# Row maxima of an attention kernel: block-diagonal matmuls become row tiles, and the spread of the inverse moves

## The reference

```
q = heads(x @ Wq.T)
k, v = heads(text @ Wk.T), heads(text @ Wv.T)
k_ip, v_ip = heads(ip @ Wk_ip.T), heads(ip @ Wv_ip.T)
out = softmax(q k^T / sqrt(32)) v + softmax(q k_ip^T / sqrt(32)) v_ip
y = merge(out) @ Wo.T + bo + x
```

## Time and profile before

| | us |
|---|---|
| median of three runs | 685.42 (683.55 to 728.46) |
| the profiled execution | 683.04 |
| its span | 681.2 |

### The profile page before, as it was taken

One profiled execution on the slowest core, in us unless ns is written; L12 is line 12 of the kernel. 1 busy time (PEld: TensorE's weight loads), 2 busy tenths in 40 slices (PEclk: granted clock), 3 DMA queues, 4 the chain that ended last, 5 costly groups with the idle time before them and its releaser, 6 DMA issues.

```text
span 681.2 us, 18904 instructions
## 1 busy us (share of the span) xinstructions
PE 657.5 (97%) x6514; PEld 564.5 (83%) x6514; DVE 435.7 (64%) x956; ACT 493.3 (72%) x1078; POOL 225.0 (33%) x261
## 2 busy tenths in 40 slices
PE   9959798999999999999999999999999999999997
PEld 9959576788888888888888888888888888888877
DVE  6786677675757566675756576665657566756633
ACT  3983787877868777877777787778777777876730
POOL 4020102243432434343434324343434243342333
PEclk9989898999999999999999999999999999999999
DMA  8950111223131221313131312213131323212212
GB/s 318 410 234 9 25 56 34 80 57 96 49 103 51 82 63 55 93 48 97 51 93 49 99 55 86 55 55 93 48 101 51 90 55 93 56 50 64 56 42 69
DMA packets 34691, 57.46 MB, mean 84 GB/s; under 512 B 4832, under 2 KB 27232, under 8 KB 34400
## 3 DMA queue, kind: packets, MB, share of 16 engines
q1 hardware_dynamic: 34656, 56.99, 27.3%
HBM read 35.34 MB, written 10.49 MB: 67 GB/s over the span
## 4 chain that ended last, share of the span: by engine, by line
PE 85%; DVE 6%; ACT 6%; issue 2%; POOL 0%; DVEq 0%; ACTq 0%
PE q_ps L711 19%; PE x_ps L711 19%; PE sum_ps L769 11%; PE b_ps L752 10%; PE pv_ps L780 10%; PE a_ps L735 7%; PE x_ps L789 5%; PE a_ps L741 1%; ACT probs L405 1%; DVE k_stack L631 1%; DVE k_stack L641 1%; ACT k_stack L485 1%; ACT q_stack L397 1%; DVE wo_lo L554 1%; DVE k_stack L545 1%
## 5 line engine op out<-in xcount | busy, mean ns | idle before, releaser
L405 ACT ACTIVATE probs<-b_ps 77x512 f32<-77x512 f32 x320 | 181.1, 591 | 121.0 <-PE b_ps L752 119.3
L562 DVE TENSOR_TENSOR q_stack<-q_ps,q_hi 32x256 fp32r<-32x256 f32 x320 | 134.3, 420 | 36.0 <-ACT q_hi L390 32.3
L571 DVE TENSOR_REDUCE row_max<-a_ps 128x4 f32<-128x308 f32 x320 | 137.6, 471 | 24.0 <-PE a_ps L735 21.3
L397 ACT ACTIVATE q_stack<-q_hi 32x256 fp32r<-32x256 f32 x320 | 133.0, 416 | 10.0
L598 DVE TENSOR_TENSOR scaled<-x_ps,pv_sb 128x512 f32<-128x512 f32 x75 | 51.9, 692 | 105.4 <-PE x_ps L789 105.0
L752 PE MATMUL b_ps<-q_stack,k_stack 98*77 98x256 f32 x640 | 115.1, 281 | 0.5 <-ACT probs L405 0.5
L347 POOL TENSOR_TENSOR scaled<-scaled 128x256 f32<-128x256 f32 x80 | 59.2, 740 | 139.1 <-DVE scaled L598 139.0
L352 POOL TENSOR_TENSOR attn_lo<-scaled,attn_hi 128x256 fp32r<-128x256 f32 x80 | 59.1, 739 | 113.2 <-ACT attn_hi L434 113.2
L358 POOL TENSOR_TENSOR res<-y,res 128x256 f32<-128x256 f32 x70 | 51.1, 731 | 136.8 <-ACT y L428 136.8
L735 PE MATMUL a_ps<-k_diag,q_hi 128*128 128x308 f32 x320 | 87.3, 313 | 7.0 <-DVE row_max L571 6.8
L752 PEld LDWEIGHTS b_ps<-q_stack,k_stack 98*77 98x77 f32 x640 | 85.7, 146 | 1.5 <-ACT probs L405 1.0
(11 more groups left out here) (111 smaller groups left out, 962.3 us busy)
## 6 DMA issues: line engine op xcount, KB each, us to landing
x_raw<-x_in SPq DMA_DIRECT2D x16, 640.0 KB, 4.2
q_stack<-q_stack SPq DMA_DIRECT2D x80, 128.0 KB, 2.3
res<-x_in SPq DMA_DIRECT2D x75, 128.0 KB, 2.0
y_out<-res SPq DMA_DIRECT2D x75, 128.0 KB, 1.7
stage<-wk_in SPq DMA_DIRECT2D x6, 640.0 KB, 7.9
...
```

Source lines behind the costliest of these rows:

```text
L397: done = nc.scalar.activation(q_stack[0:D, u.slot, j, :], q_hi[j * D:(j + 1) * D, u.slot, :].bitcast(F32), ACT.Copy)
L405: nc.scalar.activation(probs[0:KEYS, j, :], b_ps[j % 2][0:KEYS, :], ACT.Exp).then_inc(b_drained, 1)
L562: done = nc.vector.tensor_tensor(q_stack[D:2 * D, u.slot, j, :], q_ps[rows, 0:N], q_hi[rows, u.slot, :].bitcast(F32), ALU.subtract)
L571: nc.vector.tensor_reduce(row_max[:, u.slot, br, :, sub], bank[:, 0:BLK].rearrange("p (j n) -> p j n", j=GROUP), AXIS.X, ALU.max).then_inc ...
```

## The change

The block-diagonal keys are replaced by `k_heads`, in which each head keeps its own 32 rows, with the 77 keys of both branches side by side. The maxima of a unit become eight matmuls of 154 columns: for each half of the queries four, one a head, each on its own row tile of 32 rows and into its own PSUM bank (b_ps0, b_ps1, a_ps0, a_ps1). They stand at the end of a unit, behind the weighted values, for the unit two ahead. VectorE reduces a bank at a time, at the start of its unit, ahead of `normalise`. The query projection is cut into pieces of 5, 3, 4 and 3 steps between the scores. The transposition and then the spread (now into a_ps1) follow the last score, ahead of the output projection. `normalise` and POOL's `add_branches` take the unit five back in place of six; ScalarE's four exponentials stand together behind `keep_pv`, `keep_sums` and `attn_high`.

```diff
-BLK = GROUP * KEYS
+BLK = BRANCHES * KEYS
...
-MAXES = SUB * BRANCHES
-A_ITEMS = MAXES + 1
+MAX_ITEMS = GROUP + 1
...
-        k_diag = sbuf("k_diag", [P, BRANCHES, GROUPS, BATCHES, GROUP, KEYS], F32R)
+        k_heads = sbuf("k_heads", [P, GROUPS, BATCHES, BRANCHES, KEYS], F32R)
...
+        max_banks = [*b_ps, *a_ps]
...
-                ahead, norm, chunk = u.tile_plus(1), u.plus(-1 - SPREAD_LAG), u.plus(-OUT_LAG)
+                ahead, norm, chunk = u.tile_plus(1), u.plus(-SPREAD_LAG), u.plus(-OUT_LAG)
+                if norm.plus(-1).exists():
+                    attn_low(norm.plus(-1))
                 if norm.exists():
                     add_branches(norm)
-                    attn_low(norm)
...
                 before, ahead, nxt = u.tile_plus(-1), u.tile_plus(2), u.plus(2)
                 norm, chunk = u.plus(-1 - SPREAD_LAG), u.plus(-OUT_LAG)
-                exp(u, 0)
-                exp(u, 1)
                 if u.plus(-1).exists():
                     keep_pv(u.plus(-1))
                 if u.g == 0 and before.exists():
                     keep_sums(before)
-                exp(u, 2)
                 if norm.exists():
                     attn_high(norm)
-                exp(u, 3)
+                for j in range(GROUP):
+                    exp(u, j)
                 if nxt.exists():
                     q_high(nxt)
                     q_top(nxt)
...
-                for j in range(GROUP):
-                    rows = slice(j * D, (j + 1) * D)
-                    done = nc.scalar.activation(
-                        k_diag[rows, br, g, :, j, :],
-                        k_banks[br][g % 2][rows, group_cols(g)].rearrange("p (b n) -> p b n", b=BATCHES),
-                        ACT.Copy, scale=SCALE)
-                done.then_inc(k_hi_done, 1)
+                nc.scalar.activation(k_heads[:, g, :, br, :],
+                                     k_banks[br][g % 2][:, group_cols(g)].rearrange("p (b n) -> p b n", b=BATCHES),
+                                     ACT.Copy, scale=SCALE).then_inc(k_hi_done, 1)
...
-            def max_piece(u, k):
-
-                sub, br = divmod(k, BRANCHES)
-                wait(dve, a_ready, u.number(A_ITEMS, k + 1))
-                bank = a_ps[(u.c * A_ITEMS + k) % 2]
-                nc.vector.tensor_reduce(row_max[:, u.slot, br, :, sub],
-                                        bank[:, 0:BLK].rearrange("p (j n) -> p j n", j=GROUP), AXIS.X,
-                                        ALU.max).then_inc(a_drained, 1)
+            def max_piece(u, j, bank):
+
+                if not (u.fixed and u.number() == 0):
+                    wait(dve, max_ready, u.number(1, 1))
+                nc.vector.tensor_reduce(row_max[:, u.slot, :, j, :].rearrange("p r s -> p s r"),
+                                        bank[:, 0:SUB * BLK].rearrange("p (s r n) -> p s r n", s=SUB, r=BRANCHES),
+                                        AXIS.X, ALU.max).then_inc(max_read, 1)
 
             def max_turned(u):
 
-                wait(dve, a_ready, u.number(A_ITEMS, A_ITEMS))
+                wait(dve, max_turned_over, u.number(1, 1))
                 wait(dve, max_in[u.slot], u.uses_of_slot(DMA) - DMA)
                 nc.vector.tensor_copy(max_rows[:, u.slot, :],
-                                      a_ps[(u.c * A_ITEMS + MAXES) % 2][0:BRANCHES * SUB * GROUP, 0:P]).then_inc(a_drained, 1)
+                                      a_ps[0][0:BRANCHES * SUB * GROUP, 0:P]).then_inc(max_read, 1)
...
-            def normalise(u, bank=x_ps):
+            def normalise(u, bank=a_ps[1]):
...
             def emit(u):
-                norm, nxt = u.plus(-1 - SPREAD_LAG), u.plus(1)
-                if norm.exists():
+                norm, nxt = u.plus(-SPREAD_LAG), u.plus(1)
+                if nxt.exists():
+                    if not (u.fixed and u.number() == 0):
+                        for j in range(GROUP):
+                            max_piece(nxt, j, max_banks[j])
+                    max_turned(nxt)
+                if norm.exists() and u.g != 0:
                     normalise(norm)
-                if nxt.exists():
-                    for k in range(MAXES):
-                        max_piece(nxt, k)
-                    max_turned(nxt)
                 if u.g == 0 and u.tile_plus(-1).exists():
                     invert_sums(u.tile_plus(-1))
+                if norm.exists() and u.g == 0:
+                    normalise(norm)
                 if u.plus(2).exists():
                     q_low(u.plus(2))
...
-            def max_scores(u, k):
-
-                sub, br = divmod(k, BRANCHES)
-                if k == 0:
-                    wait(pe, q_hi_done, u.number(1, 1))
-                wait(pe, a_drained, u.number(A_ITEMS, k - 1))
-                nc.tensor.matmul(a_ps[(u.c * A_ITEMS + k) % 2][:, 0:BLK], q_hi[:, u.slot, sub * P:(sub + 1) * P],
-                                 k_diag[:, br, u.g, u.batch].rearrange("p j n -> p (j n)"),
-                                 start=True, stop=True).then_inc(a_ready, 1)
+            def max_matmuls(u, heads, banks):
+
+                for sub in range(SUB):
+                    for j, bank in zip(heads, banks):
+                        rows = slice(j * D, (j + 1) * D)
+                        done = nc.tensor.matmul(bank[:, sub * BLK:(sub + 1) * BLK],
+                                                q_hi[rows, u.slot, sub * P:(sub + 1) * P],
+                                                k_heads[rows, u.g, u.batch].rearrange("p r n -> p (r n)"),
+                                                start=True, stop=True, skip_group_check=True)
+                return done
+
+            def max_scores(u):
+
+                wait(pe, q_hi_done, u.number(1, 1))
+                wait(pe, max_read, u.number(MAX_ITEMS))
+                wait(pe, scaled_done, u.number(1, -1 - SPREAD_LAG))
+                max_matmuls(u, range(GROUP), max_banks).then_inc(max_ready, 1)
 
             def turn_maxima(u):
-                wait(pe, a_drained, u.number(A_ITEMS, MAXES))
-                nc.tensor.transpose(a_ps[(u.c * A_ITEMS + MAXES) % 2][0:BRANCHES * SUB * GROUP, 0:P],
-                                    row_max[:, u.slot].rearrange("p r j s -> p (r j s)"), ident[:]).then_inc(a_ready, 1)
+                wait(pe, max_read, u.number(MAX_ITEMS, GROUP))
+                nc.tensor.transpose(a_ps[0][0:BRANCHES * SUB * GROUP, 0:P],
+                                    row_max[:, u.slot].rearrange("p r j s -> p (r j s)"), ident[:]
+                                    ).then_inc(max_turned_over, 1)
...
                     wait(pe, max_in[u.slot], u.uses_of_slot(DMA))
+                if j < 2 and u.plus(1).exists():
+                    wait(pe, max_read, u.number(MAX_ITEMS, MAX_ITEMS + j + 1))
                 wait(pe, b_drained, u.number(GROUP, j - 1))
...
                 wait(pe, scaled_done, u.number())
-                wait(pe, y_done, u.number(1, 1 + SPREAD_LAG - OUT_LAG))
-                spread_matmuls(u, x_ps)
+                if u.plus(SPREAD_LAG + 1).exists():
+                    wait(pe, max_read, u.number(MAX_ITEMS, (SPREAD_LAG + 1) * MAX_ITEMS + GROUP))
+                spread_matmuls(u, a_ps[1])
 
             def project_out(c):
 
-                wait(pe, scaled_done, c.number(1, OUT_LAG - SPREAD_LAG))
+                wait(pe, y_done, c.number())
                 out_chunk(c, x_ps)
 
...
-
-                def find_max(k):
-                    if nxt.exists():
-                        max_scores(nxt, k) if k < MAXES else turn_maxima(nxt)
-
-                find_max(0)
-                find_max(1)
+                project_q(u.plus(2), 0, 5)
                 scores(u, 0)
+                project_q(u.plus(2), 5, 8)
                 scores(u, 1)
-                project_q(u.plus(2), 0, 8)
-                find_max(2)
+                project_q(u.plus(2), 8, 12)
                 scores(u, 2)
-                find_max(3)
-                project_q(u.plus(2), 8, 10)
+                project_q(u.plus(2), 12)
                 scores(u, 3)
-                project_q(u.plus(2), 10, 13)
-                find_max(MAXES)
-                project_q(u.plus(2), 13)
+                if nxt.exists():
+                    turn_maxima(nxt)
+                if norm.exists():
+                    spread_inverse(norm)
                 if chunk.exists():
                     project_out(chunk)
                 row_sums(u)
                 weigh_values(u)
-                if norm.exists():
-                    spread_inverse(norm)
+                if u.plus(2).exists():
+                    max_scores(u.plus(2))
...
-            max_scores(first, 0)
-            max_scores(first, 1)
+            wait(pe, q_hi_done, 1)
+            max_matmuls(first, (0, 1), a_ps).then_inc(first_max_ready, 1)
             project_ip_values(4, 5)
-            max_scores(first, 2)
-            max_scores(first, 3)
+            wait(pe, max_read, 2)
```

(4 more changed lines are left out.)

29 lines of the change are left out of this document (14 added, 15 removed).

## The result

| | before | after |
|---|---|---|
| median | 685.07 us (4 runs, 683.55 to 728.46) | 783.57 us (4 runs, 781.88 to 786.82) |
| profiled execution, span | 683.04, 681.2 | 781.88, 780.0 |

The change makes the kernel slower: the ratio is 1.145, with a 95% interval of 1.140 to 1.151. One of the four executions of the kernel before, 728.46, fell in a slower state and is not in the ratio. The prediction had the direction and, of the mechanisms, the largest one, but 735 us and an upper end of 770 are both too low.

The account below looks back on a forecast made before the run. TensorE, busy 97% of the span, was taken to bound the steady part. 683 - 4 (prologue) - 2 (first ten units) - 13 (maxima) + 47 (spread) + 3 (third score) + 21 (clock) = 735 us, range 705 to 770.

Parts of the forecast that it names:

- the term of -2 for the first ten units: First ten units, bound by ScalarE and VectorE: their order shortens a little, 2 us saved (0 to 5).
- nothing, as long as these margins of 0.05 us and more hold: Moved waits in an ordinary unit: each result is ready before TensorE needs it, so no cost.
- Maxima: Maxima block on TensorE: 0.56 us removed, 0.18 added plus 0.20 for leaving row tiles; 13 us saved over 70 units.
- The first is the thinnest: Margin at a unit's first score: maxima piece read at 0.65 us, score stands at 0.7; each 0.1 us is 8 us.
- The spread in mid-unit: In a tile's first unit TensorE's spread waits 3.15 us for VectorE's inverse of the sums, 15 times: 47 us.
- The clock after such a wait: After each wait for the inverse TensorE's granted clock drops: 1.4 us for 15 tiles, 21 us, bounds 0 and 26.
- Rival A: The clock holds at the stalls where the spread waits: 714 us in place of 735; chance 0.14.
- The third score of a tile's first unit: A tile's first exponential comes 0.4 us late behind ScalarE's split of x; third score waits 0.2, 15 times: 3 us.
- The prologue: Before the first units: fewer ScalarE copies for scaled keys, TensorE's wait for x_lo ends near 43; 4 us saved.
- Rival C: In the maxima block, row tiles load one after another: 0.84 us for 0.18, total 781 us; chance 0.11.

Follow-up runs that it names:

- run 4: The kernel after the change, loop kept, with the inverse of the sums made for the first tile only and used for all: 706.74 us, ratio 1.036.
- Runs 9: The kernel after, loop written out, inverse for the first tile only, six projection steps ahead of the first score instead of five: 684.61 us, ratio 1.001.
- 10: The kernel after, loop written out, inverse for the first tile only, seven projection steps ahead of the first score instead of five: 683.17 us, ratio 1.000.
- run 7: The kernel after, loop written out, with the spread of a tile's first unit moved back behind the weighted values and normalise behind q_low: 708.63 us, ratio 1.037.
- Runs 1: The kernel after the change with its loop of six passes written out, nothing else changed: 758.65 us, ratio 1.111.
- 5: The kernel before the change with twenty long-fulfilled waits (ten instructions) added to TensorE's queue in each looped unit: 753.91 us, ratio 1.102.
- 6: The kernel after, second branch's weighted values in one full matmul, with the first head's probabilities for all four heads: 775.93 us, ratio 1.137.
- Run 11: The kernel after, loop written out, inverse for the first tile only, with wo_lo behind the maxima in VectorE's first units: 681.60 us, ratio 0.997.
- run 3: The kernel before the change with eight long-fulfilled waits added in each looped unit: four executions of 694.70, 700.37, 717.04 and 717.40 us, no ratio.

## Why the prediction was wrong

The step that failed first is one that the prediction does not have. Its sum, 683 - 4 - 2 - 13 + 47 + 3 + 21, has no term for TensorE's return to the head of the loop: it counted what stands in TensorE's queue, put the return at nothing without a reason, and never asked how long the queue of a pass may be. The runs showed five jumps at 5.25 us, 26 us in all. The step that failed next is the term of -2 for the first ten units, which measured about +5.6. The step after that is "nothing, as long as these margins of 0.05 us and more hold", which measured 0.19 us a unit. Around these, the sum against the measurement (all of the profiled executions, 683.0 to 781.9; the first row sums start at 68.33 after and 70.41 before, those of the eleventh unit at 155.21 and 141.05):

| stretch | predicted | measured | missed |
|---|---|---|---|
| up to the first row sums | -4 | -2.1 | 1.9 |
| the first ten units (with two inverse waits and their clock) | +7.5 | +16.3 | 8.8 |
| the rest: ordinary units, 13 inverse waits, jumps | +48.5 | +84.6 | 36.1 |

- **Maxima.** Right for the block: 0.17, and 0.2 behind it. The term of -13 was still about twice too large: an ordinary unit went from 7.47 to 7.38, a tile without waits takes 36.9 (run 4) against 37.38, some 6 us in 70 units. Two things that the sum lacks stand behind that, and it is luck that they partly cancel. Before, the spread behind the column tiles took 0.35 and the transposition 0.11; now the two stand together between other matmuls and take 0.35 in all: 0.11 gained. The thin margin lost 0.19. So -0.56 + 0.39 - 0.11 + 0.19 = -0.09.
- **"The first is the thinnest".** The margin was named and even priced (8 us for each 0.1), but set at 0.05 by leaving out the way to TensorE. It cost 0.19 a unit in the loop form, 13 us in 70 units, of which 6 show as a miss (7.38 instead of the 7.30 of the sum), since the spread gained the others. Runs 9 and 10 give 9.2 and 10.7 back in the written-out form, where it cost 0.30 a unit.
- **The spread in mid-unit.** Right in place, cause and size (3.15 predicted; 47.2 us in 15 waits measured, 3.15 each). Run 4 and run 7 show it to be the largest loss.
- **The clock after such a wait.** Nearly right for a wait that stands alone: in a tile without jump the first unit takes 12.2, that is 4.8 over an ordinary one, 3.09 of it idle, so 1.7 of clock against my 1.4. Rival A, the clock holds, is refuted: it dropped behind 14 of the 15 waits. Short in sum, because there are more waits than I knew, and a drop behind a jump's wait and one behind the inverse wait 4 us later lie in the same unit. In all 106 us ran at the lower level, 17 before: 89 more at half the speed, up to 45 us, against the 21 of the sum.
- **The third score of a tile's first unit.** The 3 us put for it did not show: in the loop of run 4, first units without a jump take 7.39 to 7.40 like all others.
- **The jump.** No term. Five jumps at 5.25 are 26 of the 36.1 us missed in the rest; the ordinary units are 6 to 7 more, the last units about 2, and about 1 has no place. Runs 1, 5 and 6 show the cause. The new order adds about nine records a unit, which could be counted beforehand; where the limit lies could not.
- **The first ten units.** "Their order shortens a little: 2 us" was an argument from order alone. Units 1 to 4 take 34.7 us instead of 29.4, and the other ordinary ones 0.3 more, so the term of -2 measured +5.6. Waits of the scores for the maxima, 10.5 us, stand there now, where 6.4 stood before. Run 11 shows the cause: with `wo_lo` behind the maxima, units 1 to 4 take 25.1. The other 1.2 of the 8.8 missed are in the two units with an inverse wait.
- **The prologue.** The wait for x_lo ended at 43.60, near the predicted 43; but the first row sums came only 2.1 us sooner. Waits that the kernel before does not have stand between: 1.02 us for VectorE's reading of the first maxima (54.02), 0.35 for the same (65.30) and 0.57 for the first exponentials (68.32).
- **Rival C** gave 781 and its mechanism is refuted. A total that fits is no evidence for the way to it.

Not settled: where between 1729 and 1776 records the jump becomes long; what run 3's longer executions had; and why the same wait of 3.07 us drops the clock at some places and not at others, which makes the cost of such a wait 3.3 to 5.8 us (run 1), not one number.
